# Position outermost in the carry of a two-stream scan convolution, and shorter chains for its statistics

## The reference

```python
x = x + _L0_conv_ref(_gn(x), centers, spreads, bias)   # positions mixed by a softmax map, 4 heads
x = x + _L1_conv_ref(_gn(x), W)                         # scan over the 64 rows of the height

def _gn(v, G=32, eps=1e-05):                            # group norm over (h, n, 2 channels)
    ...
    return ((g - m) / jnp.sqrt(s + eps)).reshape(v.shape)

# _L0_conv_ref
out = jnp.einsum('mns,bwnvs->bwmvs', posmap, xr)        # posmap: softmax over n, for 4 heads s
out = out + token_proj_n_bias[None, :, :, :, None]

# _L1_conv_ref, K = 9 taps along the position, 64 channels in and out
def step(carry, row):
    new = row + jax.nn.relu(conv1d_same(carry, W))
    return (new, new)
_, outs = jax.lax.scan(step, row0, rows[1:])
```

## Time and profile before

| | |
|---|---|
| median of 3 runs | 808.22 us |
| profiled execution | 805.2 us |
| its span, first to last instruction | 803.4 us |
| TensorE busy | 713.4 us, 89% |
| VectorE busy | 609.6 us, 76% |
| ScalarE busy | 448.1 us, 56% |
| POOL busy | 446.3 us, 56% |
| mean granted clock of TensorE | 0.975 of full |

### The profile page before, as it was taken

How to read it: one execution, slowest core, us unless ns; L and a number is a source line. 1 busy time by engine, 2 the same in 40 slices (tenths; PEclk the granted TensorE clock), 3 DMA queues, 4 the chain that set the end, 5 groups by cost and what they waited for, 6 DMA issues and landing times.

```text
span 803.4 us, 17933 instructions
## 1 busy us (share of the span) xinstructions
PE 713.4 (89%) x5290; PEld 678.5 (84%) x5290; DVE 609.6 (76%) x1393; ACT 448.1 (56%) x854; POOL 446.3 (56%) x416
## 2 busy tenths in 40 slices
PE   1567867776999999999999999998899999999996
PEld 1456655556999899999999999898899999999996
DVE  7699999994677868787887878666667676777774
ACT  2165565566566666665766676656545454544441
POOL 1767777772556656565666665564354444444443
PEclk9999899997999999999999999999999999999999
DMA  9854444311434444344434441212244444444444
GB/s 182 155 122 105 106 108 107 75 40 40 99 78 94 100 96 100 80 95 94 105 85 91 98 106 43 51 40 53 41 77 71 74 70 76 68 76 68 77 69 77
DMA packets 307599, 68.14 MB, mean 85 GB/s; under 512 B 274772, under 2 KB 307540, under 8 KB 307540
## 3 DMA queue, kind: packets, MB, share of 16 engines
q1 hardware_dynamic: 255316, 61.15, 37.2%
q10 hardware_dynamic: 52224, 6.30, 5.1%
HBM read 33.85 MB, written 33.55 MB: 84 GB/s over the span
## 4 chain that ended last, share of the span: by engine, by line
PE 73%; DVE 16%; issue 4%; POOL 3%; ACT 2%; DVEq 0%; ACTq 0%; POOLq 0%
PE ps_conv L1036 38%; PE ps_conv L1040 18%; PE ps_mix L952 8%; PE ps_in L965 4%; DVE st L711 4%; DVE st L593 3%; PE ps_out L1028 3%; DVE dev L656 2%; POOL xs L379 2%; DVE x_sb L704 1%; PE ps_small L942 1%; ACT x_paired L469 1%; ACT rows L491 1%; DVE dev L661 1%; DVE st L605 1%
## 5 line engine op out<-in xcount | busy, mean ns | idle before, releaser
L410 POOL TENSOR_TENSOR total<-x_paired,carry 128x256 f32<-128x256 f32 x256 | 201.7, 788 | 264.1 <-DVE carry L812 135.9
L521 ACT ACTIVATE carry_h<-carry 128x256 fp32r<-128x256 f32 x252 | 105.8, 420 | 230.1 <-DVE carry L812 188.9
L1036 PE MATMUL ps_conv<-carry_h,wh 128*128 128x256 f32 x1280 | 213.7, 298 | 5.2 <-ACT carry_h L521 5.2
L469 ACT ACTIVATE x_paired<-ps_in,shift 64x512 f32<-64x512 f32 (+1 forms) x256 | 174.8, 683 | 77.9 <-PE ps_in L965 74.9
L379 POOL TENSOR_TENSOR xs<-x_sb,rstd 128x512 f32<-128x512 f32 x104 | 194.9, 1897 | 38.4 <-DVE rstd L686 38.4
L822 DVE TENSOR_TENSOR carry_l<-carry,carry_h 128x256 fp32r<-128x256 f32 x252 | 151.3, 600 | 64.3 <-ACT carry_h L521 55.4
L1036 PE MATMUL ps_conv<-carry_h,wl 128*128 128x256 f32 x1280 | 197.8, 285 | 0.0
L1040 PE MATMUL ps_conv<-carry_l,wh 128*128 128x256 f32 x1280 | 196.6, 284 | 0.0
L1036 PEld LDWEIGHTS ps_conv<-carry_h,wh 128*128 128x128 f32 x1280 | 176.4, 192 | 7.2 <-ACT carry_h L521 5.8
L1036 PEld LDWEIGHTS ps_conv<-carry_h,wl 128*128 128x128 f32 x1280 | 174.0, 191 | 0.0
L812 DVE SCALAR_TENSOR_TENSOR carry<-ps_conv,rows 128x256 f32<-128x256 f32 x256 | 107.0, 418 | 86.3 <-PE ps_conv L1040 81.1
(11 more groups left out here) (93 smaller groups left out, 412.3 us busy)
## 6 DMA issues: line engine op xcount, KB each, us to landing
x_sb<-in_x_dram SPq DMA_DIRECT2D x52, 512.0 KB, 4.1
out_dram<-staged SPq DMA_DIRECT2D x128, 128.0 KB, 2.4
out_dram<-staged SPq DMA_DIRECT2D x320, 32.0 KB, 1.5
rows<-in_x_dram SPq DMA_DIRECT2D x12, 512.0 KB, 4.0
out_dram<-staged ACTq DMA_DIRECT2D x192, 32.0 KB, 1.7
x_paired<-in_L_conv_W_dram SPq DMA_DIRECT2D x2, 80.0 KB, 2.7
x_paired<-in_L_conv_W_dram SPq DMA_DIRECT2D x2, 64.0 KB, 2.5
x_paired<-v_attention_centers_dram SPq DMA_DIRECT2D x1, 0.0 KB
```

Source lines behind the costliest of these rows:

```text
L410: nc.gpsimd.tensor_tensor(total[s][:, :].rearrange("p (w j) -> p w j", w=WS), x1_rows(wave, it, i, 1, s * WS, WS)[:, 0, :, :], carry[s][:, ...
L469: ins = nc.scalar.activation(dst[q * C:(q + 1) * C, r:CR:2, :], src[:, q, :, :], ACT.Identity, bias=shift1[r * C:(r + 1) * C, k:k + 1])
L521: nc.scalar.activation(carry_h[s][:, :, EDGE:EDGE + J], carry[s][:, :].rearrange("p (w j) -> p w j", w=WS), ACT.Copy).then_inc(high_ready[ ...
L1036: nc.tensor.matmul(ps_conv[:, s * BANK:s * BANK + SW], w[:, d, :], carry_h[s][:, :, d:d + J], start=(w is wh and d == 0), stop=False)
```

## The change

The two parts are independent of each other in what they compute; the results are the same numbers but for rounding.

**Layout.** rows, carry, carry_h, carry_l and with them ps_conv have the position pair outside and the stream's four batches innermost: carry_h is [P, 68, 4]. A tap's moving operand becomes the 256 contiguous elements from pair d on. ScalarE's norm_rows writes at a stride of four elements; POOL's total reads carry at a stride of four elements; total itself and all that follows keep their layout.

**Statistics.** dev2, square1, dev_c2 (instead of var_p) and shift2 are made by ScalarE (Square, and Copy with a scale). m2 and var1 fall away: the matmuls of var1_of and var2_of take two sources each, adding in PSUM, and EPS is added in ScalarE's Sqrt (as bias) and in ratio1. ratio1 is written to PSUM. rstd1 and the mean are kept negated (so mix is negated too). In wave 0 the chain runs earlier: mean1_of in step 5 instead of 6, dev at the end of step 5, var1_of in step 6 behind stream 0, guess1 in step 6, ratio1 and rstd1 at step 7 gap 0, mean_rstd1 at gap 2, shift1_of in step 7 instead of step 0 of the next iteration. The bn_stats of steps 4 and 5 are dealt out anew.

```diff
-        carry_h = [sb(f"carry_h{s}", [P, WS, JP], f32r) for s in range(NS)]
-        carry_l = [sb(f"carry_l{s}", [P, WS, JP], f32r) for s in range(NS)]
+        carry_h = [sb(f"carry_h{s}", [P, JP, WS], f32r) for s in range(NS)]
+        carry_l = [sb(f"carry_l{s}", [P, JP, WS], f32r) for s in range(NS)]
...
-                                        carry[s][:, :].rearrange("p (w j) -> p w j", w=WS),
+                                        carry[s][:, :].rearrange("p (j w) -> p w j", w=WS),
                                         ALU.add).then_inc(total_ready[s], 1)
...
+            def dev2_of(b, halves=1):
+                act.wait_ge(dev_ready, b + 1)
+                nc.scalar.activation(dev2[:, 0:halves, :], dev[:, 0:halves, :], ACT.Square,
+                                     scale=math.sqrt(COUNT // halves)).then_inc(dev2_ready, 1)
+
+            def std1_of(b, halves=1):
+                act.wait_ge(var1_in_ps, b + 1)
+                act.wait_ge(consts, 1)
+                nc.scalar.activation(std1[:, :], var1_ps, ACT.Sqrt, bias=eps_col[:, 0:1],
+                                     scale=float(halves) / COUNT).then_inc(std1_ready, 1)
+
+            def square1_of(b, halves=1):
+                act.wait_ge(guess1_ready, b + 1)
+                nc.scalar.activation(square1[:, :], guess1[:, :], ACT.Square,
+                                     scale=math.sqrt(0.5 * halves / COUNT)).then_inc(square1_ready, 1)
+
+            def dev_c2_of(b):
+                act.wait_ge(dev_c_ready, b + 1)
+                nc.scalar.activation(dev_c2[:, :], dev_c[:, :], ACT.Square).then_inc(dev_c2_ready, 1)
+
+            def shift2_of(b):
+                act.wait_ge(rstd2_ready, b + 1)
+                act.wait_ge(minus_mean2_ready, b + 1)
+                nc.scalar.activation(shift2[:, bass.ds(b, 1)], minus_mean2[:, :], ACT.Copy,
+                                     scale=rstd2[:, bass.ds(b, 1)]).then_inc(shift2_ready, 1)
...
-                nc.scalar.activation(rows[:, g % 2, :, w, :], x1_rows(wave, it, g * RG, RG, w, 1)[:, :, 0, :],
+                nc.scalar.activation(rows[:, g % 2, :, w // WS, :, w % WS], x1_rows(wave, it, g * RG, RG, w, 1)[:, :, 0, :],
...
             for b in range(W):
                 if b > 0:
                     keep_in(b - 1, (b - 1) % 2, 0, b - 1, CH - 1, 0, 4, None)
+                dev2_of(b + 1)
                 keep_in(b, b % 2, 0, b, 0, 0, 4, None)
+                if b > 1:
+                    shift2_of(b - 2)
                 std1_of(b + 1)
+                square1_of(b + 1)
                 keep_in(b, b % 2, 0, b, 1, 0, 4, None)
+                if b > 0:
+                    dev_c2_of(b - 1)
                 keep_in(b, b % 2, 0, b, 2, 0, 4, None)
...
-            for w in range(W):
+            for w in range(W - 1):
                 first_rows(1, w)
+            dev_c2_of(B - 1)
+            shift2_of(B - 1)
+            first_rows(1, W - 1)
...
-                average(var1_ps, weights, [dev[:, half, :] for half in range(halves)], var1_in_ps)
+                pe.wait_ge(dev2_ready, b + 1)
+                average(var1_ps, weights, [st1[:, half, :, 2] for half in range(halves)]
+                        + [dev2[:, half, :] for half in range(halves)], var1_in_ps)
...
-                        nc.tensor.matmul(ps_conv[:, s * BANK:s * BANK + SW], w[:, d, :], carry_h[s][:, :, d:d + J],
+                        nc.tensor.matmul(ps_conv[:, s * BANK:s * BANK + SW], w[:, d, :], carry_h[s][:, d:d + J, :].rearrange("p j w -> p (j w)"),
                                          start=(w is wh and d == 0), stop=False)
```

More of the change, by code:

```diff
@@ L1 @@
+import math
 import concourse.bass as bass
@@ L553, in _ @@
             keep_in(W - 1, 1, 0, W - 1, CH - 1, 0, 4, None)
-            for w in range(W - 2, W):
-                first_rows(0, w)
+            shift2_of(W - 2)
+            first_rows(0, W - 2)
+            dev_c2_of(W - 1)
+            shift2_of(W - 1)
+            first_rows(0, W - 1)
             for e in range(2):
@@ L744, in prep @@
                     stats2(b - 1, 1, bw - 1, 2, 0)
-                if i == 1 and gap == 0 and prev:
-                    keep_shift1(b, e)
+                if i == 5 and gap == 3 and more:
+                    dev_of(b + 1)
                 if i == 2 and gap == 1 and prev:
@@ L985, in var2_of @@
             def var2_of(b, wave):
[L986 to L987 removed]
+                pe.wait_ge(dev_c2_ready, b + 1)
+                pe.wait_ge(minus_mean2_ready, b + 1)
+                average(var2_ps[wave], group_avg[:, :, :, :].rearrange("p q g e -> p (q g e)"),
+                        [mv[:, 1:2], dev_c2[:, :]], var2_in_ps)
             def prep(b, e, i, after, prev, more):
@@ L999, in prep @@
                         turn_in(b - 1, 1 - e, CH - 1)
-                        shift1_of(b)
+                    if i == 5 and more:
+                        if prev:
+                            pe.wait_ge(var2_ready, b)
+                        mean1_of(b + 1, inv_p[:, :], 1)
+                    if i == 7 and more:
+                        shift1_of(b + 1)
                     if i % 2 == 0 and i > 0:
```

165 lines of the change are left out of this document (61 added, 104 removed).

## The result

The changed kernel takes 785.84 us (median of 4 runs, 785.44 to 792.56) against 808.12 us of the kernel before (4 runs); the ratio is 0.976 [0.973, 0.979]. The forecast was 761 us. It is faster, but by 22 us and not by 47; 785.84 lies at the very end of the stated range, 745 to 786.

What follows compares the result with a forecast made beforehand. VectorE was taken to bound the alone stage, TensorE's convolution matmuls waves 0 and 1. -17 (alone), -17.8 (wave 0), -14.8 (wave 1), +2.1 and +0.5 (turns) sum to -47.0: 761 us, range 745 to 786.

Steps and rivals of the forecast that it cites:

- Taps, the main term: Convolution matmuls on TensorE: contiguous operands bring each from 0.121 to 0.1115 us, 0.29 us a step of 30.
- Taps at 0.117: Rival on the convolution matmuls: weight load or the like, not row breaks, holds taps 0 and 4; 779 us, chance 0.18.
- ScalarE's rows: Rows written by ScalarE at 16-byte stride: extra cost between 0 and 0.51 us, taken as 0.
- POOL's total: POOL's sum reading carry at 16-byte stride: rises by 0.21 us, from 0.74 to 0.95.
- Wave 1: Second TensorE stage: a loop through other engines bounds the step at 3.40 us instead of 3.635; 14.8 us off.
- Wave 0: First TensorE stage: -18.1 cheaper matmuls, -4.2 stall on dev, +3.1 averages, +1.4 wait for mean_rstd1; -17.8 us.
- the stalls on dev: Wave 0: TensorE's stall on dev, 4.2 us in the stage, goes as VectorE's two-source steps leave the chain.
- the signs of being wrong: Closing list of what would refute the forecast, among them TensorE waiting over 0.3 us for dev2 or mean_rstd1.
- The forecast wait: Wave 0, step 7: shift1_of waits on TensorE for VectorE's mean_rstd1, about 0.2 us x 7 = 1.4 us.
- The alone stage: Stage from 31 to 190 us, bound by VectorE: 2.4 us off each of seven batches, 17 us in all.
- The rival of 12 us less: The stage before wave 0 passes to POOL and ScalarE's queue, gaining 12 us less: 773 us, chance 0.13.
- The turn: Start of wave 1: dev_c2 stands behind seven rows in ScalarE's queue, so the first carry comes 2.1 us later.

Runs made afterwards that it cites:

- sizes: Changed kernel with part of the convolution left out: five low-weight matmuls take 192 columns, five of carry_l 128, instead of 256; 771.19 us, one run.
- low_bf16: Changed kernel with carry_l and the weights of its five convolution matmuls in bf16, square1 kept in std1's place; 785.38 us, ratio 0.9735.
- turn_early: Changed kernel with dev_c2_of(B - 1) behind the third of wave 1's seven first rows instead of behind the seventh; 784.59 us, ratio 0.972.

## Why the prediction failed, step by step

**Taps, the main term: mis-sized.** The step that failed is "since a load starts just after the matmul before it, I take 0.11 and a little: 0.1115". The two bounds were right, and sizes and low_bf16 measured each by itself, 0.111 and 0.109. (That a mixing matmul of the earlier trace rows is two passes, from which I had the 0.109 before, is a reading that no run shows; low_bf16 has the figure for one matmul.) I took the greater of the two floors for the result. It is 0.118, my upper bound, which the earlier trace rows had shown for taps 0 and 4. That reading, the rival "Taps at 0.117", is the one that came true for the taps; I had given it 0.18, since I could not name what would hold the engine there, and I still cannot. The gain is 30 x 0.003 = 0.09 us a step and not 0.29. In wave 0 the convolutions of an iteration give 1.2 us (0.8 in layout_only, which has the new layout alone) where 2.3 were forecast, 8 us short over seven; in wave 1 TensorE alone needs 3.54 us a step where the loop was to give 3.40, 9 us short over 63. That is 17 of the 27 us missing; of the other 10, 4 are in wave 1 too, 2 in wave 0's first seven iterations, 3.5 in its last one and the turn, and 1 ahead of wave 0. The Trainium skill (TensorE: Matmul & The Clock Gate, Back-to-back issue gap) gives 109 ns for 256 columns for a matmul by itself, and says that with a weight load for each matmul the two together set the spacing. The bf16 matmuls, with their loads, come out at 0.109 even so, the f32r ones at 0.118.

**ScalarE's rows: a cost set to nothing.** "I take 0" with a bound of 0.51 us beside it. It is 0.26 us, and it came due at the turn, where the prediction itself had priced it, at 3.6 us by the upper bound (it is about 1, see below). For wave 1 I wrote "ScalarE has room even so", from its busy time, 111 of 234 us, and did not count the queue: two carry_h, two rows and 1.39 us of DMA issues in a step. Rows of 0.84 us leave 0.29 us of 3.53 over. That this costs the time in wave 1 fits the loop's end but was not shown by itself.

**POOL's total: right in kind.** 0.95 forecast, 0.86 measured alone. The way from carry of stream 0 to carry of stream 1 is 2.02 us; 1.90 before, 2.11 forecast. The Trainium skill's rule (GPSIMD Engine Reference, Performance pitfalls for Q7 kernels), one cycle more an element, gives an estimate of 0.74 + 0.21 = 0.95 us; the trace shows 0.86, rather more than half of that rise.

**Wave 1: -14.8 forecast, -1.8 measured.** The tap price above, and with it a bound that is not TensorE's. At 0.118 TensorE alone would give 3.54 us a step, 6 us less than before; of these 6 only 1.8 are left, since eight steps carry 0.5 us that are not TensorE's. In before they were hidden behind 0.1212 a matmul (eight steps of 29.1 us are 240 of them). layout_only, with the same 28.87 us, shows that it comes with the layout and not with the statistics.

**Wave 0: -17.8 forecast.** Of seven iterations: the stalls on dev go as forecast; TensorE's idle time there falls from 4.2 to 1.3 us, and the four long iterations (45.5 to 47.6 us) become 43.0 to 44.8, 7.8 us less together. The other three lose 1.6 of that again, since one of them had been short (42.7 us, behind the longest). An undisturbed one falls only from 44.49 to 44.35. The convolutions give 1.2 us of it (30.9 to 29.7 summed over the starts); the averages take back 0.5, as forecast (0.44), and a wait for dev2 0.4 that I had in no sum, only among the signs of being wrong: dev2 stands in ScalarE's queue behind keep_in. The forecast wait was one for mean_rstd1, and it isn't there.

**The alone stage: right.** 17.03 us a batch against 17.1. VectorE's busy time in a batch falls from 18.7 to 19.8 us, 19.1 on the mean, to 16.4, by 2.7 where I had 2.6 with the wait inside L656 as the largest part; neither POOL nor ScalarE's queue is late. The rival of 12 us less did not come. The trace of before also bears out what that wait was for: all seven L656 that meet one of POOL's xs end 0.05 us behind the end of an xs, and the one of the stage that meets none takes 0.19 us. L656 beside xs, then alone:

```profile
154.99 1.80 POOL L379 TENSOR_TENSOR xs<-rows,rstd 128x512 f32<-128x512 f32 x1
...
154.72 2.12 DVE L656 TENSOR_TENSOR dev<-dev 128x32 f32<-128x32 f32 x1
...
37.02 0.19 DVE L656 TENSOR_TENSOR dev<-dev 128x32 f32<-128x32 f32 x1
```

**The turn: +3.4 against +2.1.** The mechanism (dev_c2 behind seven rows) was right, and turn_early confirms it; of the missing 1.3 us the longer rows are some 0.9 (layout_only). The forecast had the loss by dev_c2 on the table; three lines moved win 2.0 us of it back. The last iteration of wave 0 should have given 2 us against it and gave nothing: from its first carry to mv it is 47.9 us before and 48.0 after. With the layout alone it is 47.1 and with the statistics alone 48.7, so the new statistics cost it 0.7 us there; why stays open.

## What to carry to other kernels

Two floors under one instruction (streaming its columns, loading its weights) need not give the greater of the two; take the pitch that the trace shows where both are at work, even when nothing explains it. A transposed access between layouts is paid by some engine: price it on the engine that gets it, count that engine's whole queue (its DMA issues too) over one turn of the loop, and never enter it at nothing. When small work moves onto a queue of long instructions, put it ahead of them as soon as its input is there.
